# Delta rule on one core: projections and turnings in other gaps of a head's four stages, and the inverse's corner block on two array tiles

## What is computed

```
mixed = x @ w_qkv;  z = x @ w_z
mixed = silu(causal_conv4(mixed));  q, k, v = split(mixed)      # 16 key heads, 32 value heads, width 128
q = l2norm(q) * 128**-0.5;  k = l2norm(k)
for each token:  S = S*exp(g);  S += k (v - k.S) b;  o = q.S
y = rmsnorm(o * silu(z)) * norm_w @ w_out
```

## Time and profile before

| what | us |
|---|---|
| median of 3 runs | 5766.71 |
| profiled execution | 5765.86 |
| its span, first to last instruction | 5764.1 |
| TensorE busy | 4946.6 (86%) |
| VectorE busy | 3368.9 (58%) |
| ScalarE busy | 2579.5 (45%) |
| GpSimd busy | 1321.8 (23%) |
| mean granted TensorE clock | 0.914 |

### The profile page before, as it was taken

How to read it: one execution, slowest core, us unless ns; L and a number is a source line. 1 busy time by engine, 2 the same in 40 slices (tenths; PEclk the granted TensorE clock), 3 DMA queues, 4 the chain that set the end, 5 groups by cost and what they waited for, 6 DMA issues and landing times. The chain is left out here.

```text
span 5764.1 us, 125494 instructions
## 1 busy us (share of the span) xinstructions
PE 4946.6 (86%) x50206; PEld 3467.1 (60%) x50206; DVE 3368.9 (58%) x6334; ACT 2579.5 (45%) x6938; POOL 1321.8 (23%) x1478
## 2 busy tenths in 40 slices
PE   5699998999989999899996998888887894599969
PEld 4477776777767776677775555555554453355545
DVE  4477676767767677676774666545543554443231
ACT  2355555555555555455553443444441334334521
POOL 0333333333333333333331000111101210012200
PEclk7799999999999999999997999999998797778879
DMA  2000000000000000000001001000000000000000
GB/s 86 23 20 23 16 18 21 20 24 19 15 21 24 20 19 15 21 23 20 19 20 48 1 1 62 7 1 0 1 21 14 15 1 13 23 1 1 1 22 15
DMA packets 51263, 106.13 MB, mean 18 GB/s; under 512 B 12848, under 2 KB 20176, under 8 KB 49520
## 3 DMA queue, kind: packets, MB, share of 16 engines
q1 hardware_dynamic: 50672, 98.07, 5.7%
HBM read 90.43 MB, written 5.52 MB: 17 GB/s over the span
## 5 line engine op out<-in xcount | busy, mean ns | idle before, releaser
L1076 DVE SCALAR_TENSOR_TENSOR dh_kq<-bank,dh_conv_kq,dh_kq 128x511 f32<-128x511 f32 (+2 forms) x408 | 305.2, 748 | 178.8 <-ACT dh_kq L892 167.6
L1076 DVE SCALAR_TENSOR_TENSOR dh_v<-bank,dh_conv_v,dh_v 128x511 f32<-128x511 f32 (+2 forms) x384 | 285.8, 748 | 169.4 <-ACT dh_v L892 159.3
L638 PE MATMUL bank<-hT,dh_w_kq 128*128 128x512 f32 x544 | 276.7, 633 | 49.9 <-DVE dh_kq L1076 42.4
L638 PE MATMUL bank<-hT,dh_w_vz 128*128 128x512 f32 x512 | 271.1, 656 | 51.0 <-DVE dh_v L1076 51.0
L1289 POOL TENSOR_TENSOR dh_pto<-dh_qkm,dh_et 128x512 f32<-128x512 f32 x128 | 160.6, 1276 | 649.8 <-PE bank L614 649.8
L1143 DVE TENSOR_TENSOR dh_turned<-dh_turned,bank 128x256 f32<-128x256 f32 x384 | 153.8, 414 | 249.7 <-ACT dh_turned L937 248.0
L1818 PE MATMUL bank<-moe_h_split,moe_w 128*128 128x512 bf16 x1200 | 277.3, 381 | 14.4 <-PEq L89 14.4
L808 PE MATMUL bank<-dh_wo_gated,dh_ww 128*128 128x256 f32 x1040 | 266.6, 414 | 0.8 <-ACT dh_ww L983 0.8
L301 POOL TENSOR_TENSOR ln_rstd<-ln_var_eps,nhalf 128x16 f32<-128x16 f32 x8 | 23.2, 2904 | 1047.4 <-DVE ln_var_eps L291 1047.4
L650 PE MATMUL bank<-dh_w_vz,hT 128*128 128x256 f32 x1024 | 245.5, 383 | 0.0
L808 PEld LDWEIGHTS bank<-dh_wo_gated,dh_ww 128*128 128x128 f32 x1040 | 210.0, 207 | 36.7 <-issue 1.1
(11 more groups left out here) (428 smaller groups left out, 12410.9 us busy)
## 6 DMA issues: line engine op xcount, KB each, us to landing
dh_rates<-delta_rates SPq DMA_DIRECT2D x130, 256.0 KB, 3.3
dh_w_vz<-in_L_wvz SPq DMA_DIRECT2D x17, 512.0 KB, 3.3
mod_w<-in_L_wmod SPq DMA_DIRECT2D x4, 1536.0 KB, 7.1
dh_w_kq<-in_L_wkq SPq DMA_DIRECT2D x18, 256.0 KB, 2.7
dh_wo<-in_L_wo SPq DMA_DIRECT2D x16, 256.0 KB, 4.4
moe_w<-in_L_w13T SPq DMA_DIRECT2D x1, 3200.0 KB, 16.4
later_gates<-mod_gate SPq DMA_DIRECT2D x3, 1024.0 KB, 4.0
gate<-later_gates SPq DMA_DIRECT2D x6, 512.0 KB, 3.4
```

What stands on the lines that cost most here:

```text
L638: last = pe.matmul(pj_bank(n), w[:, kk, :], k.hT[:, kk, n % NB, :], start=(kk == 0), stop=(kk == KD - 1))
L1076: dve.scalar_tensor_tensor(y, pj_bank(n)[:, 0:S - i], taps(n)[:, TAPS - 1 - i:TAPS - i], y, ALU.mult, ALU.add).then_inc(s["v_cs" if i < TA ...
```

## The change

- TensorE, ScalarE and VectorE: the fillers stand in other gaps. Kind 0: projection 6 with its tap moves from ahead of the inverse to behind the qk product. Kind 2: turning 0 comes in the second gap and projection 13 in the third (they change places), turnings 1 and 2 come one gap later than projection 14 and 15 or beside them, and z 4 and 5 leave the tail. Kind 3: z 4 to 7 in the first four gaps, turning 4 in the fifth, 5 and 6 ahead of the inverse, 7 behind the qk product; on VectorE norm 7 and the query vectors come after `start_power`. Kind 1 keeps its fillers.
- Corner: head 1 uses the mirrored partitions. Its first block, its `off` and its corner product stand in the other half, so that corner_left alternates between the tiles (low rows, high columns) and (high rows, low columns), and so does corner. Both loops run over b outside and j inside, after the waits for both heads. ScalarE makes one more 64x256 copy (the second diagonal block of head 1 into c_even's low half).
- GpSimd waits for its own `off_diagonal` of head 0 before that of head 1, and for that before what follows.

```diff
@@ inverse
         for b in range(NB):
-            for j in HEADS:
-                at = halves[j]
-                last = pe.matmul(turn_bank(j)[LO, b, 0, :], c_odd[j][at, b, :], turn[j][at, TS[5], b, :], start=True, stop=True)
+            for at, j in zip(halves, HEADS):
+                last = pe.matmul(turn_bank(j)[at, b, 0, :], c_odd[j][at, b, :], turn[j][at, TS[5], b, :], start=True, stop=True)
@@ corner_left
-            for b in range(NB):
-                last = pe.matmul(turn_bank(j)[HI, b, 0, :], off[j][LO, b, :], c_even[j][LO, b, :], start=True, stop=True)
+        for b in range(NB):
+            for j in HEADS:
+                last = pe.matmul(turn_bank(j)[halves[1 - j], b, 0, :], off[j][halves[j], b, :], c_even[j][halves[j], b, :],
+                                 start=True, stop=True)
@@ corner
-            for b in range(NB):
-                last = pe.matmul(pow_bank(j)[LO, b, :], off[j][HI, b, :], ttb[j][HI, b, HI], start=True, stop=True)
+        for b in range(NB):
+            for j in HEADS:
+                moved = c_even[j][LO, b, :] if j else ttb[j][HI, b, HI]
+                last = pe.matmul(pow_bank(j)[halves[j], b, :], off[j][halves[1 - j], b, :], moved, start=True, stop=True)
@@ tensor_stage
-        if a == 3: project_z(pe, q, 6)
+        if a == 3: project_z(pe, q, 4)
...
-        if a == 2: project(pe, q, 13)
-        if a == 3: project_z(pe, q, 7)
+        if a == 2: turn_kq(pe, q, 0)
+        if a == 3: project_z(pe, q, 5)
...
-        if a == 2: turn_kq(pe, q, 0)
-        if a == 3: turn_kq(pe, q, 4)
+        if a == 2: project(pe, q, 13)
+        if a == 3: project_z(pe, q, 6)
...
-        if a == 2: project(pe, q, 14)
-        if a == 3: turn_kq(pe, q, 5)
+        if a == 2:
+            project(pe, q, 14)
+            turn_kq(pe, q, 1)
+        if a == 3: project_z(pe, q, 7)
...
         if a == 2:
-            turn_kq(pe, q, 1)
             project(pe, q, 15)
-        if a == 3: turn_kq(pe, q, 6)
+            turn_kq(pe, q, 2)
+        if a == 3: turn_kq(pe, q, 4)
...
-        if a == 0:
-            project(pe, q, 5)
-            project(pe, q, 6)
+        if a == 0: project(pe, q, 5)
-        if a == 2:
-            turn_kq(pe, q, 2)
-            turn_kq(pe, q, 3)
-        if a == 3: turn_kq(pe, q, 7)
+        if a == 2: turn_kq(pe, q, 3)
+        if a == 3:
+            turn_kq(pe, q, 5)
+            turn_kq(pe, q, 6)
         inverse(pe, t)
         kk_prod(pe, t)
         qk_prod(pe, t)
+        if a == 0: project(pe, q, 6)
-        if a == 2: project_z(pe, q, 4)
+        if a == 3: turn_kq(pe, q, 7)
         corner_left(pe, t)
         for j in HEADS: y_turn(pe, t, j)
-        if a == 2: project_z(pe, q, 5)
         corner(pe, t)
@@ first_block, diagonal, left_copy, corner_copy
-        act.activation(c_even[j][LO, :, :], turn_bank(j)[LO, :, 0, :], ACT.Copy).then_inc(hs[j]["a_t11"], 1)
+        act.activation(c_even[j][halves[j], :, :], turn_bank(j)[halves[j], :, 0, :], ACT.Copy).then_inc(hs[j]["a_t11"], 1)
+        if j:
+            last = act.activation(c_even[j][LO, :, :], pow_bank(j)[HI, :, :], ACT.Copy)
-        act.activation(off[j][HI, :, :], turn_bank(j)[HI, :, 0, :], ACT.Copy).then_inc(hs[j]["a_xs"], 1)
+        act.activation(off[j][halves[1 - j], :, :], turn_bank(j)[halves[1 - j], :, 0, :], ACT.Copy).then_inc(hs[j]["a_xs"], 1)
-        act.activation(ttb[j][LO, :, HI], pow_bank(j)[LO, :, :], ACT.Copy).then_inc(hs[j]["a_u12"], 1)
+        act.activation(ttb[j][LO, :, HI], pow_bank(j)[halves[j], :, :], ACT.Copy).then_inc(hs[j]["a_u12"], 1)
@@ vector_stage
         if a == 1: convolve(dve, q, 8)
-        if a == 2: convolve(dve, q, 13)
+        if a == 2: norms(dve, q, 0)
         for j in HEADS: grow(dve, t, 1, j)
...
         for j in HEADS: grow(dve, t, 2, j)
-        if a == 2: norms(dve, q, 0)
-        if a == 3: norms(dve, q, 4)
+        if a == 2: convolve(dve, q, 13)
...
-        if a == 3: norms(dve, q, 5)
...
-        if a == 3: norms(dve, q, 6)
         for j in HEADS: last_factor(dve, t, j)
         for j in HEADS: grow(dve, t, 4, j)
...
+        if a == 3: norms(dve, q, 4)
         if a:
             for j in HEADS: state(dve, t, j)
...
         if a == 3:
-            norms(dve, q, 7)
-            query_vectors(dve, q)
+            norms(dve, q, 5)
+            norms(dve, q, 6)
...
         for j in HEADS: start_power(dve, t, j)
+        if a == 3:
+            norms(dve, q, 7)
+            query_vectors(dve, q)
@@ off_diagonal, pool_stage
+        if j:
+            pool.wait_ge(hs[0]["p_nt"], t + 1)
-        pool.tensor_tensor(off[j][LO, :, :], kkm[LO, :, HI], et[j][LO, :, HI], ALU.mult).then_inc(h["p_nt"], 1)
+        pool.tensor_tensor(off[j][halves[j], :, :], kkm[LO, :, HI], et[j][LO, :, HI], ALU.mult).then_inc(h["p_nt"], 1)
...
         for j in HEADS: off_diagonal(pool, t, j)
+        pool.wait_ge(hs[1]["p_nt"], t + 1)
```

More of the change, by code:

```diff
@@ L991, in scalar_stage @@
         if a == 2: tap(act, q, 12)
-        if a == 3: silu_z(act, q, 6)
+        if a == 3: silu_z(act, q, 4)
         for j in HEADS: keep_power(act, t, 0, j)
@@ L996, in scalar_stage @@
         if a == 1: tap(act, q, 8)
-        if a == 2: tap(act, q, 13)
-        if a == 3: silu_z(act, q, 7)
+        if a == 2: squares(act, q, 0)
+        if a == 3: silu_z(act, q, 5)
         for j in HEADS: keep_power(act, t, 1, j)
@@ L1007, in scalar_stage @@
             silu(act, q, 12)
-            squares(act, q, 0)
-        if a == 3: squares(act, q, 4)
+            tap(act, q, 13)
+        if a == 3: silu_z(act, q, 6)
         for j in HEADS: keep_power(act, t, 2, j)
@@ L1020, in scalar_stage @@
             tap(act, q, 14)
-        if a == 3: squares(act, q, 5)
+            squares(act, q, 1)
+        if a == 3: silu_z(act, q, 7)
         for j in HEADS: keep_power(act, t, 3, j)
@@ L1032, in scalar_stage @@
             silu(act, q, 14)
-            squares(act, q, 1)
             tap(act, q, 15)
-        if a == 3: squares(act, q, 6)
+            squares(act, q, 2)
+        if a == 3: squares(act, q, 4)
         for j in HEADS: mean_sq(act, t, j)
@@ L1040, in scalar_stage @@
             silu(act, q, 4)
-            tap(act, q, 6)
         if a == 1:
@@ L1044, in scalar_stage @@
             silu_z(act, q, 3)
-        if a == 2:
-            squares(act, q, 2)
-            squares(act, q, 3)
-        if a == 3: squares(act, q, 7)
+        if a == 2: squares(act, q, 3)
+        if a == 3:
+            squares(act, q, 5)
+            squares(act, q, 6)
         for j in HEADS: first_block(act, t, j)
@@ L1051, in scalar_stage @@
         qk_copy(act, t)
+        if a == 0: tap(act, q, 6)
         if a == 1: tap(act, q, 11)
-        if a == 2: silu_z(act, q, 4)
+        if a == 3: squares(act, q, 7)
         for j in HEADS: left_copy(act, t, j)
@@ L1060, in scalar_stage @@
         if a == 1: silu(act, q, 11)
-        if a == 2:
-            silu_z(act, q, 5)
-            silu(act, q, 15)
+        if a == 2: silu(act, q, 15)
         for j in HEADS: corner_copy(act, t, j)
```

## The result

The changed kernel takes **5801.07 us** (median of four runs, 5796.1 to 5804.81). The kernel before, run beside it, takes 5761.18 us. The ratio is 1.0068, 95% interval 1.0051 to 1.0084: slower by 0.7%, where 1.0% was forecast. The profiled execution took 5802.28 us around a span of 5800.6, 36.4 us more than the profiled 5765.86 of before. All of this and more lies in the delta phase. Here is the busy time of the phase and of five stages, in the columns of the earlier trace rows.

A forecast was written before the change was run, and what follows sets the result against it. TensorE's pauses in the delta phase, paid twice through the lowered clock, were taken as the bound. Stages 0 to 3 gave -1.4 + 0 + 3.5 + 1.6 = +3.7 us a head, times 16 = +59: 5825 us, range 5738 to 5878.

The forecast's parts named there:

- The corner: corner_left and corner, alternating two tiles: 0.54 us each instead of 1.07, with the extra ScalarE copy hidden.
- Rival C: The corner's two tiles do not overlap; on the path in three stage kinds: +26 us, 5851 us; chance 0.07.
- Stage 0: Projection 6 behind the qk product: end at 44.0 us (-2.9), new 2 us pause +1.5 of clock, net -1.4 a head.
- The spell I counted at +1.5: Stage 0: most of a 3.4 us half-clock spell after the new 2 us pause, +1.5 us a head.
- Stage 1: End set by convolution 11, the silu after it and the corner copy; none moves, net 0.
- Stage 2: Convolution 13 behind the third addition delays projection 14 by 2.3 us; 47.2 us without clock (+0.8), net +3.5 a head.
- The 3.5 us pause lowers the clock surely: Stage 2's tail: TensorE's wait for the mask brings the low clock, +2.0 us a head.
- the +0.7 ahead of it: Stage 2, pause ahead of projection 14: half a chance of 1.5 us of clock on the path, +0.7 a head.
- Stage 3: Mask at 35.5 us, output product at 39.0, end 42.6, clock +1.2: 43.8 against 42.2, +1.6 a head.
- The rule against the clock terms: Skill's rule, all stages: a gap longer than 2.32 us is harmless; only the 3.5 us pause would count.
- Rival A: Only the long pause, in stage 2, costs clock: +0.3 us a head, 5771 us, no change; chance 0.15.
- Rival B: Stage 2: VectorE absorbs convolution 13's move, ending before about 18.3 us; stage 44.4 us, kernel faster at 5713; chance 0.16.
- Rival D: All clock spells are 6.8 us: +1.5 us in stages 2 and 3 each, +48, 5873 us; chance 0.12.

## Why the prediction came out as it did

The sign and the mechanism were right: a gain in stage 0, nothing in stage 1, and losses in stages 2 and 3 that are larger. The sum was +59 us; the stages give +43, the profiled executions differ by 36 and the medians by 40. Two terms were mis-sized in opposite directions, stage 2 by +1.9 us a head and stage 3 by -1.6, so that the total came as near as it did is partly luck.

**The corner** was right in its own time (forecast 0.54 us for 16 instructions; their 16 starts lie 31 ns apart, within 0.46 us) and in that its extra ScalarE copy is hidden. Alone it is worth 0.5%. Rival C is out.

**Stage 0** was right: 44.0 us without a clock term, and 43.9 in six of the inner 12; a pause of 2.0 us, and 1.94. The spell I counted at +1.5 costs 1.7 and comes in the other six. Measured -1.9 against -1.4.

**Stage 1** was right: 40.89 us before and after. That its end hangs on the corner copy behind the silu is borne out by the run that swaps the two: 39.35 us.

**Stage 2** was right up to the clock. Convolution 13 ends at 20.6 us as forecast; the pause is 2.28 us for the 2.3 forecast; the output multiply takes 1.21 us, and 1.69 in the three long stages, where it meets GpSimd (+0.6 had been put in for it over 0.69); the mask ends at 41.5 for 41.7 in the stage at 2121.32; the length is 47.14 us for 47.2. What failed is the step "The 3.5 us pause lowers the clock surely", with its +2.0, and the +0.7 ahead of it. Only three of 16 stages pay, both terms at once and then 4.2 us. In the other 13 the clock is at 1.00 in the tail, which the prediction itself had named as a sign of being wrong. In eight of these the low spell begins 36 us into the stage, under the kk and qk products, which take 3.63 us instead of 2.05. TensorE is then later at the mask's wait, which is 1.72 us instead of 3.3, and the spell has cost nothing:

```profile
1980.26 3.63 PE L614 MATMUL bank<-dh_kq 128*128 128x128 f32 x16 [1.70 <-DVE dh_S L1200]
...
1986.23 1.06 PE L619 MATMUL bank<-ident,dh_yy 128*128 128x128 f32 x8 [1.72 <-DVE dh_kkm L1119]
...
1988.12 3.69 PE L811 MATMUL bank<-dh_wo_gated,dh_ww 128*128 128x256 f32 x16 [0.22 <-ACT dh_ww L988]
```

In the remaining five the pause is 3.30 us and the clock stays at 1.00 for the whole stage; the stage at 2121.32 is one of them. So the term should have been 4.2 x 3/16 = 0.8 instead of 2.7, which is the difference between +3.5 and +1.6.

**Stage 3** was right in its parts and wrong in its base. The mask was put at 35.5 us and ends at 35.45 in the stage at 1815.22; the output product at 39.0 and starts at 39.3; without a low spell under the output product the stage lasts 42.9 for 42.6. The waits were 2.25 us for the "1.5 us or so" and 0.73 to 2.05 for the 1.9. What failed is "43.8, against 42.2": the 42.20 us are one stage of before at a clock of 0.92. Four of the inner 12 took 40.6, and the three at a round's end, less the 6.8 us in which TensorE only waits for the loop, 39.0. So I compared a new stage with one low spell of average cost against an old one with a spell of 6.8 us. Like against like it is 39.0 to 42.9 us with no spell that costs anything, 40.6 to 44.6 where one of 3.4 us lies under the output product, 42.2 to 44.9 where it is of 6.8. The inner 12 went from 41.7 to 44.2 us on average, 0.9 more than forecast. The round ends, which the prediction left out, pay most: 51.4 to 51.9 us instead of 45.6 to 45.9, since a low spell falls into their tail now and didn't before. These three stages are 18 of the 48 us, and 13 of the 24 us by which the 15 stages missed.

**The rule against the clock terms.** The clock was at 0.50 behind the 2.25 us pause of stage 3 and, in three of 16 heads, behind the 2.28 us pause of stage 2; it held through the 3.30 us pause in five. The Trainium skill (TensorE: Matmul & The Clock Gate, "Why this matters for your kernels") warns of idle gaps between matmul bursts above a length that lies between these two and the third. The trace does not agree: the low clock followed the first two in these stages, and it did not follow the third in five. Nor was my "surely" right. Counted over the runs, a pause of 1.48 us ahead of the transposes of stage 0 was followed by no low spell in the 24 inner stages of two kernels (projection 6 alone, the moves alone); one of 1.94 us by a spell in six of 12 here and in none to eight of 12 in the other kernels that have it; one of 3.30 us in stage 2 in three of eight here and in 13 of 16 with the old order of that stage. Rival A as a whole is out: low spells follow pauses far shorter than the long one, and 5771 us with no change in time is not what came.

**Rival B** failed at its own condition. Convolution 13 ended at 20.6, not by 18.3; with the one line moved the condition is met, and stage 2 comes to 44.6 us in ten heads (45.1 on average), its forecast having been 44.4. **Rival D** is out: 27 of the phase's low spells are of 3.4 us, 11 of 6.8, and three, at the round ends, of 10.2.

What stays open: why the low spell falls at 22 and 42 us into the stage in three heads, at 36 us in eight and not at all in five. The pattern repeats over the heads. What happens in one stage depends on others: with convolution 13 moved in stage 2 the spells of the inner stages 0 went, and with norm 7 moved in stage 3 six stages of kind 2 were long instead of three. No run here tells what sets it.

## What to carry to other kernels

Moving a filler moves its whole chain on every engine; before it is moved, look in each queue at what it now stands behind and who waits for its end. Here one convolution behind one addition instead of ahead of it cost 50 us, and one reduction ahead of a buffer's release 28. What no one needs in this stage belongs behind the last operation that someone waits for: moving the key vectors and one silu there gave some 51 us, as much as the best repair of the change. It has to be checked what the queue then runs into: the query vectors, moved in the same way, brought the mask forward by only 0.3 us, since the scan behind them met GpSimd. And a stage that repeats should be measured over all its repeats before one of them is taken as the base of a difference.

## What the runs showed of the hardware that I had not expected

- The same stage, instruction for instruction, takes 47.1 or 51.3 us, by where in it the granted clock is 0.50. A spell under work that has slack cost nothing (eight stages of 47.1 us). A shorter piece of work can also go with more of it: with the corner alone, stage 0 stayed at 47.0 to 47.2 us in 11 of 12, although 0.9 us of its work was gone, and its low spell was 6.8 us instead of 3.4.
- Unread matmuls in a pause made one kernel faster (ratio 1.0032 for 1.0068) and another no slower (0.9771 for 0.9792, the intervals overlapping), and took 99 and 68 us of low clock out of the phase.
- Two 64x64 tiles of the array, used in turn, start 16 instructions within 0.46 or 0.47 us in 58 of the 64 stages (in the others within 0.49 to 0.62). On one tile the 16 starts lie within 0.92 us.
- Two kinds of VectorE operation got longer where GpSimd ran its 128x512 products at the same time: the multiply of 128x512 with both operands in SBUF, 1.69 us instead of 0.69, and the two scans, 3.24 or 3.83 instead of 2.33. The multiply with an operand in PSUM stayed at 0.69 beside the same product, and in stage 2 a scan kept its 1.2 us beside the GpSimd product that writes dh_inj; so it depends on the pair. How far an operation slips into GpSimd's time is thus a price of a reordering; in the kernel with the query vectors late the scan took 1.5 us back in every stage of kind 3.
